# One-hot slot matrix of the expert stages: from GpSimd and VectorE to VectorE alone, with routing and sending two slots closer

## The chip, the cores and the metric

One Trainium2 chip, one of its cores. The metric is the device time of one execution in microseconds (us). The kernel before: median 2519.32 us of 3 executions (2517.7 to 2520.26).

## What is computed

The program is a small transformer on `x` of 32 batches x 256 tokens x 128 features: a binarised feed-forward, a gated attention unit, the same feed-forward again, a mixture of experts, a linear attention, and the mixture of experts again. The change touches the two expert stages only. Cut to what matters, per batch:

```python
logits = layernorm(x) @ router_w + router_b                  # 8 experts
top2, ei = top_k(logits, 2); p = softmax(top2)
pos = running count of tokens per expert, first choices ahead of second ones
inputs[e, pos] += token          # capacity 76 rows per expert; the rest is dropped
h = silu((inputs @ w_fc + b_fc) * (inputs @ w_gate + b_gate))
out = h @ w_proj + b_proj
x = x + 0.5 * sum over the two choices of p * out[ei, pos]
```

## The kernel before, in words

`program` runs six stages one behind the other: ffn, gau, ffn, moe, lin, moe. Within a stage five engines run instruction lists written out by hand and meet at semaphores; each engine takes its list strictly in order. VectorE, ScalarE, GpSimd and SyncE work on what TensorE makes, and a wait at the head of an engine's list holds all that stands behind it.

`moe_stage` (L1286 on) cuts the 32 batches into eight chunks of 2, 3, 5, 5, 5, 5, 5 and 2 batches (`CHUNKS`, here chunk 0 to chunk 7). All batches of a chunk go through the eight experts together, 76 columns each, so five batches make matmuls 380 wide. A chunk is eight units (experts) of four slots, 32 slots in all. In each slot TensorE runs `up` (L1531 on): four matmul instructions of the first weight (L1538) and of the gate weight (L1542), two each; ScalarE adds the first bias (`bias_fc`, L1611), VectorE adds the gate bias and multiplies (`multiply`, L1715), ScalarE takes Silu over two slots' worth (L1618). Behind the fourth slot of a unit TensorE runs `down` for the unit before it (L1552, 24 matmuls for five batches, 16 for two or three) and VectorE adds the output bias (`bias_out`, L1724). The banks for the gate result are two, so the gate matmul of a slot waits for the `multiply` of the slot two before it.

While a chunk is computed, the batches of the next one are routed, and those of the chunk before are gathered and combined. `slots_of` (L1369 on) lays this side work into the slots: batch i of the next chunk starts at slot i times 5 (9 in chunks 0 and 6), and its steps come so many slots later as `ROUTE_LAGS` says:

- norm 0: VectorE normalises (L261), and GpSimd's `split` makes three bf16 parts (L1436 to L1439);
- transpose 1 (L1493, ScalarE's copy L1588), router 2 (matmul L1500; VectorE's `choose` L1662 to L1668), mask 3 (`choose_masks`, L1678 to L1684), count 4 (matmuls L1510 to L1514);
- assign 5: VectorE's `assign` (L1691 to L1700) works out the slot number of both choices of each token (L1697 signals `routed`);
- with assign, GpSimd's `first_choice` (L1442 on, instruction L1447): for each of the two 128-token tiles a `tensor_scalar` over 608 slot numbers, 1 where the number is that of the first choice;
- hot0 at 8 and hot1 at 9: VectorE's `second_choice` (L1702 on, instruction L1705), one tile each: a `scalar_tensor_tensor` that adds the second choice to what GpSimd wrote;
- send0 at 10 and send1 at 11: TensorE's `send` (L1517 on, matmuls L1526, six for each half) moves the tokens into their slots. send0 waits for both tiles of the batch (`hot_sb`); ScalarE's `land` (L1602) copies each half out of the one bank.

In a slot VectorE's order is: multiply, norm, router, mask, assign, hot0 or hot1, combine, and bias_out at the end of a unit. TensorE's order is: up, router, transpose, count, send, down. GpSimd's order is: split, first_choice, gather. `combine` (L1733, then statistics L273) of a batch of the chunk before comes at slots 11, 17, 23 in chunk 2 and 11, 16, 21, 26, 31 in chunks 3 to 6 (14 and 20 in chunk 1), with the four indirect DMAs of its gather (L1456) five slots earlier. In chunk 7 nothing is routed. At the head of a stage chunk 0's two batches are routed with no expert work beside them.

In what follows, the slot of a batch's assign is called A, and the three slots behind it B, C and D. For batch i of chunks 1 to 5 that is A = 5 + 5i.

```python
ROUTE_LAGS = {"norm": 0, "transpose": 1, "router": 2, "mask": 3, "count": 4, "assign": 5, "hot0": 8, "hot1": 9,
              "send0": 10, "send1": 11}
...
if h == 0:
    pe.wait_ge(split_done, b + 1)
    pe.wait_ge(hot_sb, TILES * (b + 1))
```

## Time and profile before

| | us |
|---|---|
| median of 3 executions | 2519.32 |
| the profiled execution, its own time | 2514.78 |
| span of the profile | 2512.8 |
| first expert stage, from its first instruction to the statistics of its last batch | about 514 to 1080 |
| second expert stage | about 1917 to the end |

The profile lists busy time by engine, the span in slices, the chain that ended last, and groups of instructions with the idle time before them and its releaser; the trace gives the instructions in order of time. PE is TensorE, DVE VectorE, ACT ScalarE, POOL GpSimd. A number in square brackets behind an instruction is the idle time of its engine just before it, with what ended it.

### The profile page before, as it was taken

The page shows a single profiled execution, that of the slowest core. Times are in us where ns is not written, and L with a number is a line of the kernel's source. Part 1 is how long each engine was busy: PE and PEld are TensorE (multiplying, and loading weights), DVE is VectorE, ACT ScalarE, POOL GpSimd, SP SyncE. Part 2 cuts the span into 40 slices and gives each one's busy share as a digit, 9 for nine tenths or more (in the row PEclk, how much of TensorE's full clock was granted, in tenths as well). Part 3 has the DMA queues.
Part 4 walks back from the last instruction along what each step waited for, and adds up shares of the span by engine and source line. Part 5 has one row for each costly group of instructions (what it writes and reads, how often), then busy time and mean ns, then how long its engine had stood idle before and what let it go on. Part 6 is the DMA issues. An engine that isn't in the chain of part 4 may idle for free.

```text
span 2512.8 us, 47937 instructions
## 1 busy us (share of the span) xinstructions
PE 2272.8 (90%) x14854; PEld 1816.3 (72%) x14854; DVE 1588.7 (63%) x4974; ACT 1312.6 (52%) x2713; POOL 733.7 (29%) x818
## 2 busy tenths in 40 slices
PE   3979998968999999849999999999996889999994
PEld 3979997957767676637777777777775776776773
DVE  5867776766667775435655656565655666767653
ACT  3755556744444444326666666666662544444441
POOL 2202220045546765320000000000002455766543
PEclk9989999989999999879999999999998999999997
DMA  7040000000111111100000000000000001111122
GB/s 242 0 159 0 0 0 0 0 5 23 26 28 40 41 36 41 46 18 1 0 0 0 0 0 0 0 0 0 0 0 0 15 25 35 43 50 45 49 56 50
DMA packets 70867, 67.45 MB, mean 27 GB/s; under 512 B 9696, under 2 KB 58336, under 8 KB 70368
## 3 DMA queue, kind: packets, MB, share of 16 engines
q1 hardware_dynamic: 61504, 47.16, 5.9%
q0 software_dynamic: 8192, 16.79, 2.9%
q10 hardware_dynamic: 1056, 2.10, 0.3%
q8 instruction: 56, 0.92, 0.2%
q14 instruction: 59, 0.48, 0.1%
HBM read 31.94 MB, written 34.08 MB: 26 GB/s over the span
## 4 chain that ended last, share of the span: by engine, by line
PE 48%; issue 4%; DVE 2%; POOL 1%; ACT 1%; DMA 0%; another core or an unknown queue 0%; ACTq 0%; POOLq 0%; DVEq 0%
PE moe_bank L1552 5%; PE lin_bank L983 5%; PE moe_bank L1538 5%; PE lin_bank L903 5%; PE moe_bank L1542 5%; PE lin_bank L911 4%; PE lin_bank L930 4%; PE lin_bank L922 4%; PE lin_bank L959 3%; PE lin_bank L975 2%; PE moe_bank L1526 2%; PE lin_bank L946 1%; POOL moe_landed L1456 1%; ACT lin_xT L1049 0%; PE moe_bank L1493 0%
## 5 line engine op out<-in xcount | busy, mean ns | idle before, releaser
L1611 ACT ACTIVATE moe_fc<-moe_bank,all_b_fc 128x380 f32<-128x380 f32 (+2 forms) x512 | 262.3, 513 | 341.7 <-PE moe_bank L1538 286.8
L1715 DVE SCALAR_TENSOR_TENSOR moe_act<-moe_bank,all_b_moe_gate,moe_fc 128x380 f32<-128x380 f32 (+2 forms) x512 | 271.0, 531 | 221.4 <-PE moe_bank L1542 106.9
L1538 PE MATMUL moe_bank<-moe_rowsT,all_w_fc 128*128 128x380 f32 (+2 forms) x1024 | 357.3, 431 | 15.6 <-ACT moe_fc L1611 12.8
L1542 PE MATMUL moe_bank<-moe_rowsT,all_w_gate 128*128 128x380 f32 (+2 forms) x1024 | 351.7, 425 | 12.9 <-DVE moe_act L1715 7.7
L1552 PEld LDWEIGHTS moe_bank<-all_w_proj,moe_act 128*128 128x128 f32 x2688 | 321.6, 195 | 12.4 <-ACT moe_act L1618 1.8
L1552 PE MATMUL moe_bank<-all_w_proj,moe_act 128*128 128x128 f32 x2688 | 329.2, 279 | 1.4 <-ACT moe_act L1618 1.4
L1456 POOL DMA_INDIRECT moe_landed<-rows_out,moe_take_at x256 | 266.0, 1039 | 176.2 <-issue 174.6
L1542 PEld LDWEIGHTS moe_bank<-moe_rowsT,all_w_gate 128*128 128x128 f32 x1024 | 188.3, 193 | 101.6 <-DVE moe_act L1715 8.9
L1447 POOL TENSOR_SCALAR moe_hot<-all_slot_ids,moe_slot 128x608 bf16<-128x608 f32 x128 | 233.3, 1830 | 91.7 <-issue 54.9
L1618 ACT ACTIVATE moe_act<-moe_act 128x760 f32<-128x760 f32 (+2 forms) x256 | 181.5, 709 | 96.0 <-DVE moe_act L1715 88.8
L1148 POOL COPY lin_xn_ones<-lin_xn 128x254 f32<-128x254 f32 x32 | 12.7, 398 | 748.0 <-PE lin_bank L911 743.3
L1053 ACT ACTIVATE lin_neg<-lin_bank 128x512 f32<-128x512 f32 x256 | 151.7, 592 | 95.3 <-PE lin_bank L903 50.7
L1538 PEld LDWEIGHTS moe_bank<-moe_rowsT,all_w_fc 128*128 128x128 f32 x1024 | 167.9, 193 | 43.6 <-ACT moe_fc L1611 13.5
L959 PEld LDWEIGHTS lin_bank<-lin_kv,lin_qT 128*128 128x128 f32 x1024 | 144.4, 191 | 63.4 <-issue 54.1
L1057 ACT ACTIVATE lin_neg<-lin_neg 128x512 f32<-128x512 f32 x256 | 161.1, 630 | 7.9
L1526 PE MATMUL moe_bank<-moe_hot,moe_parts 128*128 128x304 bf16 x768 | 125.5, 301 | 40.4 <-issue 24.7
L1081 ACT ACTIVATE lin_gate_tanh<-lin_bank,all_bg_half 128x256 f32<-128x256 f32 x256 | 103.5, 468 | 108.3 <-PE lin_bank L930 108.2
L1724 DVE TENSOR_TENSOR moe_expert_out<-moe_bank,all_b_proj 128x384 f32<-128x384 f32 (+1 forms) x128 | 64.8, 506 | 142.9 <-PE moe_bank L1552 108.4
L959 PE MATMUL lin_bank<-lin_kv,lin_qT 128*128 128x130 f32 x1024 | 151.9, 275 | 1.1 <-DVE lin_heads L1196 0.8
L1526 PEld LDWEIGHTS moe_bank<-moe_hot,moe_parts 128*128 128x128 bf16 x768 | 72.5, 100 | 96.3 <-issue 69.1
L903 PE MATMUL lin_bank<-all_wk,lin_xT 128*128 128x512 f32 x256 | 128.9, 607 | 4.5 <-ACT lin_xT L1049 2.7
L451 ACT ACTIVATE ffn_hT<-ffn_bank,all_b,all_alpha 128x256 f32<-128x256 f32 x256 | 123.6, 564 | 17.2 <-PE ffn_bank L407 17.2
(222 smaller groups left out, 4309.2 us busy)
## 6 DMA issues: line engine op xcount, KB each, us to landing
rows_out<-moe_expert_out SPq DMA_DIRECT2D x80, 128.0 KB
rows_out<-all_zeros SPq DMA_DIRECT2D x1, 9728.0 KB, 28.0
rows_out<-moe_expert_out SPq DMA_DIRECT2D x80, 62.0 KB
moe_landed<-rows_out,moe_take_at POOLq DMA_INDIRECT x256
out<-all_x SPq DMA_DIRECT2D x5, 640.0 KB
rows_out<-moe_expert_out SPq DMA_DIRECT2D x48, 64.0 KB
all_w_fc<-in_w_fc SPq DMA_DIRECT2D x1, 2048.0 KB, 9.8
all_w_gate<-in_w_gate SPq DMA_DIRECT2D x1, 2048.0 KB, 13.7
```

The costliest lines, as they stand in the source:

```text
L903: nc.tensor.matmul(bank[j][:, :], xT[:, j // 2 * P:(j // 2 + 1) * P], k.wk[:, j % 2 * HU:(j % 2 + 1) * HU], start=True, stop=True).then_in ...
L959: last = nc.tensor.matmul(bank[4 + n % 2][:, i * 2 * DH1:(i + 1) * 2 * DH1], qT[:, p, t * P:(t + 1) * P], kv[:, p, :], start=True, stop=True)
L1057: nc.scalar.activation(neg[:, j, :], neg[:, j, :], ACT.Exp, scale=-1.0).then_inc(exps.sem, 1)
L1447: nc.gpsimd.tensor_scalar(hot[:, b % 2, t, :], k.slot_ids[:, :], slot[:, b % 2, t, 0:1], None, ALU.is_equal).then_inc(hot_first, 1)
L1456: nc.gpsimd.indirect_dma_start(landed[:, b % LANDED, t, h, :], None, k.rows_out, bass.IndirectOffsetOnAxis(take_at[:, i, h:h + 1], 0), bou ...
L1526: last = nc.tensor.matmul(bank[SENT][:, 0:HALF], parts[:, b % PARTS, q, t, :], hot[:, b % 2, t, h * HALF:(h + 1) * HALF], start=(t == 0 an ...
L1538: nc.tensor.matmul(bank[FC + j % 2][:, 0:c.width], k.w_fc[:, e, j * P:(j + 1) * P], rowsT[:, c.n % 2, e, 0:c.width], start=True, stop=True ...
L1542: nc.tensor.matmul(bank[GATE + j % 2][:, 0:c.width], k.w_gate[:, e, j * P:(j + 1) * P], rowsT[:, c.n % 2, e, 0:c.width], start=True, stop= ...
L1552: last = nc.tensor.matmul(bank[OUT][:, j * DIM:(j + 1) * DIM], act_in[:, i % 2, h, j * P:(j + 1) * P], k.w_proj[:, e * MC + h, :], start=( ...
L1611: nc.scalar.activation(fc[:, j, 0:c.width], bank[FC + j % 2][:, 0:c.width], ACT.Identity, bias=k.b_fc[:, e * MC + j:e * MC + j + 1]).then_ ...
L1618: nc.scalar.activation(a, a, ACT.Silu).then_inc(act_sb, 1)
L1715: nc.vector.scalar_tensor_tensor(act_in[:, i % 2, j, 0:c.width], bank[GATE + j % 2][:, 0:c.width], k.b_moe_gate[:, e * MC + j:e * MC + j + ...
```

## The change

`first_choice` leaves GpSimd, with its semaphore. VectorE makes each tile whole: a `tensor_scalar` for the first choice, a wait for its own result, and the `scalar_tensor_tensor` as before. The lags of hot0, hot1, send0 and send1 fall from 8, 9, 10, 11 to 6, 7, 8, 9.

```diff
-ROUTE_LAGS = {... "assign": 5, "hot0": 8, "hot1": 9,
-              "send0": 10, "send1": 11}
+ROUTE_LAGS = {... "assign": 5, "hot0": 6, "hot1": 7,
+              "send0": 8, "send1": 9}
...
-                def first_choice(b):
-                    pool.wait_ge(routed, b + 1)
-                    if b >= 2:
-                        pool.wait_ge(sent_ps, 2 * (b - 2) + 2)
-                    for t in range(TILES):
-                        nc.gpsimd.tensor_scalar(hot[:, b % 2, t, :], k.slot_ids[:, :], slot[:, b % 2, t, 0:1], None,
-                                                ALU.is_equal).then_inc(hot_first, 1)
...
                     dve.wait_ge(chosen, b + 1)
                     if b >= 2:
-                        dve.wait_ge(hot_first, TILES * (b - 1))
...
-                def second_choice(b, t):
-                    dve.wait_ge(hot_first, TILES * b + t + 1)
+                def choices(b, t):
                     dve.wait_ge(routed, b + 1)
+                    if b >= 2:
+                        dve.wait_ge(sent_ps, 2 * (b - 2) + 2)
+                    link(nc.vector.tensor_scalar(hot[:, b % 2, t, :], k.slot_ids[:, :], slot[:, b % 2, t, 0:1], None, ALU.is_equal))
                     nc.vector.scalar_tensor_tensor(hot[:, b % 2, t, :], k.slot_ids[:, :], slot[:, b % 2, t, 1:2], hot[:, b % 2, t, :],
                                                    ALU.is_equal, ALU.add).then_inc(hot_sb, 1)
```

The calls of `first_choice` at the head of the stage and with every assign go too, and those of `second_choice` become `choices`. `link` makes VectorE wait for the instruction just issued.

## Rows read from the trace of the kernel before

**Rows 1.** The page, busy time of three engines (share of the span) and instructions.

```profile
PE 2272.8 (90%) x14854; PEld 1816.3 (72%) x14854; DVE 1588.7 (63%) x4974; ACT 1312.6 (52%) x2713; POOL 733.7 (29%) x818
```

**Rows 2.** Busy time in windows, chunk 3, from multiply of A to multiply of D.

```profile
core 0: us, PE busy (x) PEld busy (x) DVE busy (x) ACT busy (x) POOL busy (x), PEclk, DMA share, GB/s
739.25:746.68 7.43, 7.42 (x43) 5.50 (x42) 4.95 (x21) 3.57 (x6) 5.77 (x6) 1.00 0.01 3
749.71:758.88 9.17, 8.99 (x55) 7.01 (x56) 7.20 (x28) 4.18 (x8) 8.37 (x9) 1.00 0.18 42
...
776.66:783.38 6.72, 6.72 (x38) 4.86 (x37) 6.41 (x27) 3.65 (x7) 5.20 (x6) 1.00 0.10 29
788.17:796.49 8.32, 8.32 (x49) 6.25 (x50) 5.54 (x19) 4.02 (x7) 6.84 (x6) 1.00 0.13 28
```

**Rows 3.** Timeline of DVE, slots A to D of batch i = 3.

```profile
776.66 0.61 DVE L1715 SCALAR_TENSOR_TENSOR moe_act<-moe_bank,all_b_moe_gate,moe_fc 128x380 f32<-128x380 f32 x1 [0.82 <-PE moe_bank L1542]
777.19 0.60 DVE L261 TENSOR_SCALAR moe_xn<-all_x,moe_mean,moe_rstd 128x128 f32<-128x128 f32 x2
...
779.32 0.61 DVE L1715 SCALAR_TENSOR_TENSOR moe_act<-moe_bank,all_b_moe_gate,moe_fc 128x380 f32<-128x380 f32 x1
779.85 1.82 DVE L1733 SCALAR_TENSOR_TENSOR all_x<-moe_landed,moe_prob,all_x 128x128 f32<-128x128 f32 x4
...
782.10 0.60 DVE L1715 SCALAR_TENSOR_TENSOR moe_act<-moe_bank,all_b_moe_gate,moe_fc 128x380 f32<-128x380 f32 x1
...
783.38 0.59 DVE L1715 SCALAR_TENSOR_TENSOR moe_act<-moe_bank,all_b_moe_gate,moe_fc 128x380 f32<-128x380 f32 x1
```

**Rows 4.** Timeline of PE beside it: gates of A and D, one send.

```profile
775.72 0.80 PE L1542 MATMUL moe_bank<-moe_rowsT,all_w_gate 128*128 128x380 f32 x2
...
778.63 0.94 PE L1526 MATMUL moe_bank<-moe_hot,moe_parts 128*128 128x304 bf16 x6
...
781.76 0.80 PE L1542 MATMUL moe_bank<-moe_rowsT,all_w_gate 128*128 128x380 f32 x2
```

**Rows 5.** Instructions by tile (ns min/median/max), and the page's group of bias_out.

```profile
L1447 POOL TENSOR_SCALAR moe_hot<-all_slot_ids,moe_slot x128: 1790/1812/2090, 527.9 to 2401.1; 128x608 bf16<-128x608 f32 x128
L1705 DVE SCALAR_TENSOR_TENSOR moe_hot<-all_slot_ids,moe_slot,moe_hot x128: 836/844/1355, 529.8 to 2406.9; 128x608 bf16<-128x608 f32 x128
...
L773 DVE TENSOR_SCALAR gau_lin_qT<-gau_qkT,all_os_gamma,all_os_beta x33: 408/412/414, 169.4 to 386.0; 128x256 f32<-128x256 f32 x33
...
L261 DVE TENSOR_SCALAR moe_xn<-all_x,moe_mean,moe_rstd x128: 331/341/479, 520.6 to 2386.1; 128x128 f32<-128x128 f32 x128
...
L1724 DVE TENSOR_TENSOR moe_expert_out<-moe_bank,all_b_proj 128x384 f32<-128x384 f32 (+1 forms) x128 | 64.8, 506 | 142.9 <-PE moe_bank L1552 108.4
```

**Rows 6.** Timeline of DVE: a combine with no first_choice beside it.

```profile
691.71 1.25 DVE L1733 SCALAR_TENSOR_TENSOR all_x<-moe_landed,moe_prob,all_x 128x128 f32<-128x128 f32 x4
```

**Rows 7.** Busy time in windows: batch i = 3 of chunk 1, batch 0 of chunk 0.

```profile
626.32:633.12 6.80, 4.67 (x30) 3.77 (x29) 6.26 (x27) 2.99 (x7) 6.38 (x7) 1.00 0.15 38
...
547.48:550.99 3.51, 3.51 (x31) 3.43 (x30) 2.46 (x12) 1.89 (x5) 1.98 (x2) 1.00 0.01 2
```

**Rows 8.** Timeline of PE: three waits in chunk 1, with what followed the first.

```profile
613.51 1.31 PE L1526 MATMUL moe_bank<-moe_hot,moe_parts 128*128 128x304 bf16 x6 [2.24 <-issue]
614.61 3.26 PE L1552 MATMUL moe_bank<-all_w_proj,moe_act 128*128 128x128 f32 x16
...
622.84 2.03 PE L1552 MATMUL moe_bank<-all_w_proj,moe_act 128*128 128x128 f32 x16
...
2017.90 0.94 PE L1526 MATMUL moe_bank<-moe_hot,moe_parts 128*128 128x304 bf16 x6 [2.18 <-issue]
...
2036.39 0.65 PE L1542 MATMUL moe_bank<-moe_rowsT,all_w_gate 128*128 128x228 f32 x2 [3.39 <-DVE moe_act L1715]
```

**Rows 9.** Busy time in a window behind the first of these waits.

```profile
614.00:616.00 2.00, 2.00 (x11) 1.80 (x10) 1.97 (x8) 0.92 (x2) 0.00 (x0) 0.50 0.03 8
```

**Rows 10.** Timeline of PE: the first send of the stage.

```profile
533.04 1.68 PE L1526 MATMUL moe_bank<-moe_hot,moe_parts 128*128 128x304 bf16 x6 [6.01 <-DVE moe_hot L1705]
```

More of the change, by code:

```diff
@@ L1262 @@
 COMBINE_IN = {1: (14, 6), 2: (11, 6), 3: (11, 5), 4: (11, 5), 5: (11, 5), 6: (11, 5), 7: (12, 6)}
-ROUTE_LAGS = {"norm": 0, "transpose": 1, "router": 2, "mask": 3, "count": 4, "assign": 5, "hot0": 8, "hot1": 9,
-              "send0": 10, "send1": 11}
+ROUTE_LAGS = {"norm": 0, "transpose": 1, "router": 2, "mask": 3, "count": 4, "assign": 5, "hot0": 6, "hot1": 7,
+              "send0": 8, "send1": 9}
 GATHER_LEAD = 5
@@ L1341, in moe_stage @@
         routed = k.sem("routed")
-        hot_first = k.sem("first_choice_hot")
         hot_sb = k.sem("hot_ready")
@@ L1467, in _ @@
                     split(b)
-                for b in plan[0].batches:
-                    first_choice(b)
                 for c, slots in order:
@@ L1473, in _ @@
                             split(work["norm"])
-                        if "assign" in work:
-                            first_choice(work["assign"])
                         if "gather" in work:
@@ L1746, in _ @@
                     for t in range(TILES):
-                        second_choice(b, t)
+                        choices(b, t)
                 dve.wait_ge(cleared, 1)
@@ L1762, in _ @@
                             if f"hot{t}" in work:
-                                second_choice(work[f"hot{t}"], t)
+                                choices(work[f"hot{t}"], t)
                         if "combine" in work:
```

## The prediction

> **What bounds the kernel now.** I read the page first: TensorE is busy 90% of the span, VectorE 63%, GpSimd 29% [rows 1]. So a whole-span view says that VectorE has room and GpSimd more. But the change puts work into particular slots, so what counts is which engine is behind in those. I took windows of chunk 3 that run from the multiply of slot A to that of slot D, four of its five routed batches [rows 2] (the fifth, i = 2, is like i = 1). TensorE is busy in all of them nearly without a gap (8.99 of 9.17 us, 6.72 of 6.72): any wait that it gets there is added to the time one for one. The granted clock is 1.00, that is 2.4 GHz. VectorE is busy 4.95, 7.20, 6.41 and 5.54 us in the same windows, on the bare busy count.
>
> Then the timeline of batch 3 [rows 3, 4]. VectorE's multiply of A starts at 776.66, 0.14 us after the gate matmul of A ends (775.72 + 0.80). It works from there to 783.38 with no idle time, and at D it is already behind: TensorE's gate of D ended at 782.56. Today that costs nothing, since nothing at D needs VectorE at once; its two hots come in D and E and the send in the next A.
>
> **What the change moves.** send0 moves from the next A to D, and it needs both tiles of the batch, which VectorE now makes in B and C, at the full price of two instructions. All that VectorE has in A, B and C stands ahead: multiply, norm, assign; multiply, first tile, combine with statistics; multiply, router, second tile. TensorE goes from the gate of A to send0 with two sends fewer, as those moved on to D and E. So per batch two sums are compared, and where VectorE's is the longer TensorE waits.
>
> VectorE's additions, per tile. The `scalar_tensor_tensor` takes 0.84 us [rows 5], of which the next instruction overlaps some 0.08 (multiply at 776.66 lasts 0.61, the next starts at 777.19) [rows 3]: 0.76. The `tensor_scalar` of 608 elements on VectorE is not in the trace. Nearest rows: `tensor_scalar` of 128 elements takes 0.341 us and of 256 elements 0.412 [rows 5], so 0.55 ns an element and 0.61 us for 608. Those have two per-partition operands and this one has one, so I take 0.58, and 0.04 for the wait on its own result. The other end is 0.84, the `scalar_tensor_tensor` over the same 608. Together 1.38 us a tile, 2.76 a batch, the new one 1.24 of it.
>
> The slope of 0.55 ns is half the cycle-per-element cost that separates the two instruction kinds here. The Trainium skill (VectorE: DVE Perf Modes, section "The perf-mode tier table") has fp32 `tensor_scalar` from SBUF to SBUF at 2 elements a cycle and two-tensor operations at 1. By that page's overhead figure of about 150 cycles the tile's `tensor_scalar` would be an estimated 0.47 us, and the sum below some 12 us smaller; the rows have no instruction that short at this size.
>
> What VectorE gets back: GpSimd's two instructions of 1.81 us a batch [rows 5] run beside the combine today. The combine of batch 3 takes 1.82 us [rows 3], one with none beside it 1.25 [rows 6]: 0.5 us back in B. Against it, GpSimd's split (norm's consumer) is still running when B begins, and the first `tensor_scalar` can be held by it; bounds 0 and the 0.6 us by which the combine was held, I take 0.4 (0.25 for i = 2, where the addition of the output bias comes between).
>
> Now the sums for chunks 2 to 5, in us. VectorE before is the busy time plus 0.3 for the short gaps between linked instructions (6.72 less 6.41). Added are 2.76, 0.14 for the start, the 0.4, less the 0.5; in i = 0 and i = 4 the addition of the output bias, 0.5 [rows 5], falls behind the second tile and is taken off; i = 0 has no combine, and i = 4 no norm and so no split. TensorE is the window less 1.88 for two sends of 0.94 [rows 4] (i = 0 has none of them).
> - i = 0: 5.2 - 0.5 + 3.3 = 8.0 against 7.4: wait 0.6.
> - i = 1: 7.5 + 2.8 = 10.3 against 7.3: 3.0.
> - i = 2: as i = 1, with 0.25 for the 0.4: 2.8.
> - i = 3: 6.7 + 2.8 = 9.5. TensorE from 776.52 to 782.56 is 6.04, less 1.88 is 4.2: wait 5.3. No `down` lies between A and D here; in the other four one of 2.8 us does, which is the difference.
> - i = 4: 5.8 - 0.5 + 2.9 - 0.5 = 7.7 against 6.4: 1.3.
>
> Sum 13.0, less some 0.3 for short waits that stand at sends today: 12.7 us a chunk, 4 chunks, 2 stages: **102 us**. After each send0 VectorE has only mask and multiplies until the next A, so it catches up, and the wait comes anew with each batch.
>
> Chunk 1, with 228 columns: same steps; the largest is again i = 3, whose A also has a combine: VectorE 6.26 + 2.9 = 9.2, TensorE 4.67 - 1.88 = 2.8 [rows 7], wait 6.4. The five together make 13. Today's waits there (2.24 and its clock loss, about 2 at i = 3, smaller ones; 2.18 and 3.39 in the second stage) [rows 8] are taken in by the new order, about 7: net 6 a stage, **12 us**. These rows also show the mechanism at work before the change: a combine in the slot of hot1 (14) or of assign (20) stops TensorE. Chunk 0: VectorE 2.5 + 0.3 + 2.9 = 5.7, at 0.3 less for the others, TensorE 3.5 [rows 7]: 2.0 for three batches, less 0.7 that I estimate for today's short waits there: 5.3 a stage, **11 us**. Chunk 6 has nine slots a batch and no combine ahead of the tiles: 0, at best 1 us back.
>
> Head of a stage: the first send waits 6.01 us for the matrix [rows 10], behind two tiles at GpSimd's 1.81 and one 0.84 addition, 4.5 us; now 2 x 1.4 behind both assigns: 0.9 earlier, **-2 us** in all.
>
> **Clock.** After the 2.24 us wait the granted clock was 0.50 (1.2 GHz) for some 3 us [rows 9]; the send took 1.31 us in place of 0.94 and the `down` 3.26 in place of 2.03 [rows 8]: 1.6 to 1.7 us lost. After waits of 2.18 and 3.39 us it was not: that send took its 0.94. So I charge 1.7 for each wait over 5 us, ten of them (i = 3 in chunks 1 to 5, twice): **17 us**. Bounds: nothing, and all 26 waits over 2.5 us, 44.
>
> The moved sends cost the same matmuls; GpSimd's list only gets shorter; SyncE's is untouched; ScalarE's `land` waits behind send0 and is released in time, 0.41 us before the next half needs the bank against TensorE's four `up` matmuls of 1.3. Landing two slots earlier gains nothing: no row has TensorE wait for the rows of a chunk. The dropped wait for `hot_first` was for work long done.
>
> Sum: 102 + 12 + 11 - 2 + 17 = **140 us** on the profiled execution's 2514.8, thus 2655. The median of the runs is 4.5 us above that execution, so 2659.
>
> **Rivals.**
> 1. Faster: VectorE takes the additions in its idle time (37% of the span) and what shows is GpSimd's release. It decides where VectorE's sum from A to the second tile stays under TensorE's. Then 0.5 us back in each combine is off the path, and 2 us at the heads, today's waits in chunk 1 (about 7 a stage, 14) remain: 2519 - 16 = 2503. For it: the page's shares. Against: in i = 3 VectorE is behind at D even before. The same rule of ports stands in the Trainium skill (SBUF — State Buffer, "SBUF: two separate sides"): the port pair shared by VectorE and GpSimd is held exclusively for a whole instruction; by that rule, the 1.82 against 1.25 agrees. Chance 0.04; another 0.02 that it comes out level.
> 2. The waits come, but the clock stays: 2659 - 17 = 2642. Chance 0.25.
> 3. The waits come only where no `down` lies between (i = 3), as VectorE's chain is shorter than summed by 1.5 us or more: 8 x 3.8, 2 x 5 in chunk 1, 10 for the clock: +50, 2569. Chance 0.09.
> 4. The `tensor_scalar` runs at one element a cycle, 0.84, or is held by GpSimd's gathers as long: 0.26 to 0.3 more a tile, 0.55 a batch, in 28 batches a stage: +31, 2690; with the clock's upper bound 2715. For it: two-operand instructions of this size do, and no row has a compare that writes bf16. Chance 0.18.
>
> The forecast itself has 0.42. The matrix made by VectorE is plainly in the diff, so "does nothing" is no rival.
>
> **How the numbers follow.** 2659 is the forecast's own sum. The range leaves out rival 1, the level case and most of rival 3, and runs to the upper bound of rival 4: 2595 to 2715. A measurement can tell 0.2% (5 us) from no change: faster 0.04, same 0.02, slower 0.94.
>
> **What would show it.** In the new profile TensorE's L1526 should have some 60 long waits for VectorE's hot, 5 us ones where no `down` precedes; VectorE's idle time in A to C should be gone and the combine near 1.25 us; GpSimd's busy time down by 233 us. Right about the price if the new `tensor_scalar` is 0.5 to 0.65 us. Wrong if TensorE's waits at L1526 sum to under 50 us, or if the time comes back from another place, as matmuls at the lower clock.

## The result and the profile after

| | before | after |
|---|---|---|
| median (4 executions each), us | 2519.24 (2517.7 to 2520.26) | 2672.9 (2670.31 to 2675.66) |
| profiled execution, us | 2514.78 | 2674.94 |
| its span, us | 2512.8 | 2672.8 |
| granted TensorE clock, mean | 0.967 | 0.944 |

The ratio is 1.0619, with a 95% interval of 1.0605 to 1.0633. Slower by 154 us by the medians; the two spans differ by 160.0. Forecast was 2659 in a range of 2595 to 2715: the sign, the size and the mechanism came out, with one term missing (chunk 6) and three that were off (the clock too small, chunk 2 and the waits of chunks 3 to 5 too large). That the total lies so close is in part luck.

The lines of code moved up by 9 to 14: fc L1525, gate L1529, down L1539, send L1513, multiply L1703, bias_out L1712, combine L1721, gather L1447, the counting matmul L1497. The new `tensor_scalar` on VectorE is L1692, the `scalar_tensor_tensor` behind it L1693.

The page of after, busy time by engine, and its group for the sends:

```profile
PE 2324.1 (87%) x14854; PEld 1849.5 (69%) x14854; DVE 1642.5 (61%) x5102; ACT 1312.1 (49%) x2713; POOL 506.2 (19%) x690
...
L1513 PE MATMUL moe_bank<-moe_hot,moe_parts 128*128 128x304 bf16 x768 | 143.9, 332 | 159.3 <-issue 146.0
```

Against [rows 1]: GpSimd lost 227.5 us, VectorE gained 54 (its 128 new instructions, less what the combines got back), and TensorE, with exactly the same 14854 matmuls, is busy 51 us longer. The matmuls are the same, so what grew is the time of each, and the granted clock fell from 0.967 to 0.944 on the mean. VectorE's share of the span fell, to 61%, in a kernel that it holds up: the share says nothing here.

The waits of TensorE in after (engine, line, releaser: us in total, times, longest):

```profile
PE moe_bank L1513 <- issue: 146.0, 56, 12.5
...
PE moe_bank L1513 <- DVE moe_hot L1693: 10.0, 2, 5.0
PE moe_bank L1497 <- DVE moe_mask L1666: 9.5, 10, 1.9
PE moe_bank L1529 <- DVE moe_act L1703: 9.3, 6, 2.3
```

There are the "some 60 long waits" at the send: 56 of them, which the profile books under "issue" (it names no releaser), 48 of 0.9 us or more and 8 of 0.3. That they are waits for VectorE's second tile has to be read from the timelines. The timeline of VectorE in after, slots A to D of batch i = 3 of chunk 3, which answers to [rows 3]:

```profile
807.98 0.61 DVE L1703 SCALAR_TENSOR_TENSOR moe_act<-moe_bank,all_b_moe_gate,moe_fc 128x380 f32<-128x380 f32 x1 [0.82 <-PE moe_bank L1529]
...
809.66 0.67 DVE L1681 SCALAR_TENSOR_TENSOR moe_over<-moe_top_atf,moe_over 128x4 f32<-128x4 f32 x1
...
811.00 0.61 DVE L1703 SCALAR_TENSOR_TENSOR moe_act<-moe_bank,all_b_moe_gate,moe_fc 128x380 f32<-128x380 f32 x1
811.53 0.53 DVE L1692 TENSOR_SCALAR moe_hot<-all_slot_ids,moe_slot 128x608 bf16<-128x608 f32 x1
812.09 0.85 DVE L1693 SCALAR_TENSOR_TENSOR moe_hot<-all_slot_ids,moe_slot,moe_hot 128x608 bf16<-128x608 f32 x1
812.86 1.25 DVE L1721 SCALAR_TENSOR_TENSOR all_x<-moe_landed,moe_prob,all_x 128x128 f32<-128x128 f32 x4
...
815.82 0.52 DVE L1692 TENSOR_SCALAR moe_hot<-all_slot_ids,moe_slot 128x608 bf16<-128x608 f32 x1
816.37 0.85 DVE L1693 SCALAR_TENSOR_TENSOR moe_hot<-all_slot_ids,moe_slot,moe_hot 128x608 bf16<-128x608 f32 x1
817.14 0.61 DVE L1703 SCALAR_TENSOR_TENSOR moe_act<-moe_bank,all_b_moe_gate,moe_fc 128x380 f32<-128x380 f32 x1
```

Nine microseconds with no idle time: from 807.98 to 817.22, 9.2 us, or 9.4 with the 0.14 of start that the forecast's 9.5 includes. The timeline of TensorE beside it, the gates of slots A and D and every send0 of that chunk that waited over 0.9 us, with what followed:

```profile
784.14 0.94 PE L1513 MATMUL moe_bank<-moe_hot,moe_parts 128*128 128x304 bf16 x6 [2.52 <-issue]
...
800.72 0.94 PE L1513 MATMUL moe_bank<-moe_hot,moe_parts 128*128 128x304 bf16 x6 [3.37 <-issue]
...
807.04 0.80 PE L1529 MATMUL moe_bank<-moe_rowsT,all_w_gate 128*128 128x380 f32 x2
...
811.80 0.80 PE L1529 MATMUL moe_bank<-moe_rowsT,all_w_gate 128*128 128x380 f32 x2
...
817.33 1.68 PE L1513 MATMUL moe_bank<-moe_hot,moe_parts 128*128 128x304 bf16 x6 [4.72 <-issue]
...
818.80 4.81 PE L1539 MATMUL moe_bank<-all_w_proj,moe_act 128*128 128x128 f32 x24
...
829.51 2.84 PE L1539 MATMUL moe_bank<-all_w_proj,moe_act 128*128 128x128 f32 x24
...
834.60 0.94 PE L1513 MATMUL moe_bank<-moe_hot,moe_parts 128*128 128x304 bf16 x6 [0.97 <-issue]
```

TensorE had its gates of A to D done at 812.60 and stood until 817.33, 0.11 us behind VectorE's second tile. What follows runs slow: the send 1.68 in place of 0.94, the `down` 4.81 in place of 2.84. The windows of after show why (columns as in [rows 2]; the last but two is the granted clock):

```profile
818.00:820.00 2.00, 2.00 (x10) 1.74 (x9) 0.33 (x3) 0.96 (x2) 1.39 (x3) 0.50 0.15 33
...
784.00:790.00 6.00, 5.86 (x27) 3.52 (x28) 1.58 (x7) 2.17 (x6) 0.09 (x1) 0.72 0.06 12
```

Half clock, 1.2 GHz, behind the wait of 4.72; and 0.72 on the mean over the six microseconds behind the wait of only 2.52.

**Where the time went.** A chunk with five batches behind it and five ahead, from its first multiply to that of the next, is the cleanest unit of the stage. Windows of that length, chunk 4 of the first stage, before:

```profile
806.30:883.60 77.30, 75.89 (x446) 54.52 (x445) 55.84 (x185) 36.60 (x68) 50.46 (x50) 1.00 0.14 38
```

and after:

```profile
844.20:936.40 92.20, 80.34 (x446) 57.22 (x445) 59.99 (x196) 36.71 (x68) 33.10 (x40) 0.94 0.13 32
```

The chunk grew by 14.9 us: 10.4 of it TensorE standing (11.86 against 1.41), and 4.5 the same 446 matmuls taking longer (80.34 against 75.89). By chunk, first stage, in us, from the first multiplies in the timelines:

| chunk | 0 | 1 | 2 | 3, 4, 5 | 6 |
|---|---|---|---|---|---|
| before | 45.4 | 64.2 | 78.1 | 77.3 each | 69.1 |
| after | 50.3 | 73.5 | 84.7 | 92.2 each | 82.3 |
| grown by | 4.9 | 9.3 | 6.6 | 14.9 each | 13.2 |

That is 78.7 of the 79.3 by which the first stage grew. The second grew by 78.5 in nearly the same pattern (6.4, 8.0 and 6.5 in chunks 0 to 2, 14.5 to 15.1 in chunks 3 to 5, 13.2 in chunk 6), and the first stage began 2.0 us later than in the trace of before, which the change has no part in: 79.3 + 78.5 + 2.0 is the 160 of the spans.

Chunk 6 was forecast at nothing. Its growth is for the most part one stop. Timeline of TensorE in after:

```profile
1059.19 2.84 PE L1539 MATMUL moe_bank<-all_w_proj,moe_act 128*128 128x128 f32 x24
1061.87 0.81 PE L1525 MATMUL moe_bank<-moe_rowsT,all_w_fc 128*128 128x380 f32 x2
...
1077.26 1.68 PE L1513 MATMUL moe_bank<-moe_hot,moe_parts 128*128 128x304 bf16 x6 [12.47 <-issue]
```

of VectorE:

```profile
1074.51 0.56 DVE L1712 TENSOR_TENSOR moe_expert_out<-moe_bank,all_b_proj 128x384 f32<-128x384 f32 x1 [9.34 <-remote]
```

and of ScalarE:

```profile
1074.55 1.04 ACT L1598 ACTIVATE moe_fc<-moe_bank,all_b_fc 128x380 f32<-128x380 f32 x2 [9.84 <-remote]
```

VectorE and ScalarE both stood still for more than nine microseconds, up to the same moment, and the views name no engine for it ("remote"). The semaphore events of the trace, which no view prints, do: ScalarE waited for the signal of an `up` matmul and VectorE for that of the `down`, both TensorE's. The `down` ends at 1062.03 by its record and its signal came at 1074.48, 12.45 us later; the `up` of 1061.87 ends at 1062.67 and its signal came at 1074.53. In the expert stages such a signal comes 0.014 us behind the recorded end in the median, and at most 0.015 in nine of ten. So the stop is TensorE's: its work or its signals came late, and which of the two can't be told, as the profile only models where a matmul ends. It turned into a wait of 12.47 us because VectorE's list is in order: the second tile stands behind `bias_out`, and `bias_out` waits for the `down`. The clock followed, and the send took 1.68.

On GpSimd at that time a train of sixteen indirect DMAs was going out, 1.3 us apart, from 1051.66 to 1072.55. Rows from its start and its end:

```profile
1051.66 1.03 POOL L1447 DMA_INDIRECT moe_landed<-rows_out,moe_take_at  x1 [0.77 <-POOL moe_parts L1438]
1053.00 1.00 POOL L1447 DMA_INDIRECT moe_landed<-rows_out,moe_take_at  x1 [0.30 <-issue]
...
1071.55 1.00 POOL L1447 DMA_INDIRECT moe_landed<-rows_out,moe_take_at  x1 [0.30 <-issue]
```

In the kernel before, GpSimd makes its tiles between two gathers, and for that it must first wait for VectorE's assign. Timeline of GpSimd before, chunk 6 and then chunk 7:

```profile
988.88 1.01 POOL L1456 DMA_INDIRECT moe_landed<-rows_out,moe_take_at  x1 [0.30 <-issue]
993.02 3.61 POOL L1447 TENSOR_SCALAR moe_hot<-all_slot_ids,moe_slot 128x608 bf16<-128x608 f32 x2 [3.13 <-DVE moe_slot L1697]
996.80 1.10 POOL L1456 DMA_INDIRECT moe_landed<-rows_out,moe_take_at  x1 [0.17 <-issue]
...
1011.75 1.00 POOL L1456 DMA_INDIRECT moe_landed<-rows_out,moe_take_at  x1 [0.30 <-issue]
...
1038.23 0.99 POOL L1456 DMA_INDIRECT moe_landed<-rows_out,moe_take_at  x1 [25.49 <-issue]
...
1057.76 1.00 POOL L1456 DMA_INDIRECT moe_landed<-rows_out,moe_take_at  x1 [0.30 <-issue]
```

There the longest train of chunk 6 is one of twelve (996.80 to 1012.75), and no stop comes with it (the second stage has one of 2.2 us there). But chunk 7, where nothing is routed and GpSimd has nothing to wait for, has a train of sixteen in the kernel before too, and there VectorE stops the same way:

```profile
1061.10 0.42 DVE L1724 TENSOR_TENSOR moe_expert_out<-moe_bank,all_b_proj 128x256 f32<-128x256 f32 x1 [4.58 <-remote]
```

The change took GpSimd's wait out with the work, and chunk 6 has a train of sixteen as well. Whether that is the cause, runs had to say.

### The profile page after: what moved, and what is told of

It is laid out like the page before. It is cut to its first block, busy times and chain, and to the rows that moved or that the text cites. A ratio compares the mean times of both kernels' runs of the same rounds, so it can differ in the third digit from the quotient of the medians.

```text
span 2672.8 us, 47839 instructions
## 1 busy us (share of the span) xinstructions
PE 2324.1 (87%) x14854; PEld 1849.5 (69%) x14854; DVE 1642.5 (61%) x5102; ACT 1312.1 (49%) x2713; POOL 506.2 (19%) x690
## 4 chain that ended last, share of the span: by engine, by line
PE 47%; issue 5%; DVE 2%; ACT 1%; POOL 1%; another core or an unknown queue 0%; ACTq 0%; DMA 0%; POOLq 0%; DVEq 0%
PE moe_bank L1539 6%; PE moe_bank L1525 5%; PE moe_bank L1529 5%; PE lin_bank L983 5%; PE lin_bank L903 4%; PE lin_bank L911 4%; PE lin_bank L930 4%; PE lin_bank L922 4%; PE lin_bank L959 3%; PE moe_bank L1513 3%; PE lin_bank L975 2%; PE lin_bank L946 1%; POOL moe_landed L1447 1%; PE moe_bank L1480 0%; ACT lin_xT L1049 0%
## 5 line engine op out<-in xcount | busy, mean ns | idle before, releaser
L1703 DVE SCALAR_TENSOR_TENSOR moe_act<-moe_bank,all_b_moe_gate,moe_fc 128x380 f32<-128x380 f32 (+2 forms) x512 | 271.4, 531 | 300.7 <-PE moe_bank L1529 172.3
L1525 PE MATMUL moe_bank<-moe_rowsT,all_w_fc 128*128 128x380 f32 (+2 forms) x1024 | 360.7, 435 | 16.7 <-ACT moe_fc L1598 10.9
L1529 PE MATMUL moe_bank<-moe_rowsT,all_w_gate 128*128 128x380 f32 (+2 forms) x1024 | 358.6, 433 | 11.0 <-DVE moe_act L1703 9.3
L1539 PEld LDWEIGHTS moe_bank<-all_w_proj,moe_act 128*128 128x128 f32 x2688 | 342.6, 206 | 15.3 <-ACT moe_act L1605 1.6
L1539 PE MATMUL moe_bank<-all_w_proj,moe_act 128*128 128x128 f32 x2688 | 347.6, 289 | 1.3 <-ACT moe_act L1605 0.7
L1447 POOL DMA_INDIRECT moe_landed<-rows_out,moe_take_at x256 | 275.5, 1076 | 257.3 <-issue 118.4
L1513 PE MATMUL moe_bank<-moe_hot,moe_parts 128*128 128x304 bf16 x768 | 143.9, 332 | 159.3 <-issue 146.0
L1529 PEld LDWEIGHTS moe_bank<-moe_rowsT,all_w_gate 128*128 128x128 f32 x1024 | 191.2, 196 | 101.9 <-DVE moe_act L1703 15.1
L1513 PEld LDWEIGHTS moe_bank<-moe_hot,moe_parts 128*128 128x128 bf16 x768 | 74.7, 107 | 223.6 <-issue 190.7
L1525 PEld LDWEIGHTS moe_bank<-moe_rowsT,all_w_fc 128*128 128x128 f32 x1024 | 170.7, 196 | 45.2 <-ACT moe_fc L1598 11.6
L1589 ACT COPY moe_rowsT<-moe_bank 128x304 f32<-128x304 f32 x128 | 52.8, 412 | 266.8 <-PE moe_bank L1513 256.7
L1712 DVE TENSOR_TENSOR moe_expert_out<-moe_bank,all_b_proj 128x384 f32<-128x384 f32 (+1 forms) x128 | 64.6, 504 | 175.8 <-PE moe_bank L1539 108.6
L1148 POOL COPY lin_xn_ones<-lin_xn 128x254 f32<-128x254 f32 x32 | 12.7, 398 | 748.2 <-PE lin_bank L911 743.5
L1435 POOL CAST moe_parts<-moe_xn 128x256 bf16<-128x256 f32 x64 | 25.5, 398 | 643.8 <-DVE moe_xn L261 351.4
## 6 DMA issues: line engine op xcount, KB each, us to landing
all_w_gate<-in_w_gate SPq DMA_DIRECT2D x1, 2048.0 KB, 13.2
```

Of the source, the lines that this page charges most:

```text
L1447: nc.gpsimd.indirect_dma_start(landed[:, b % LANDED, t, h, :], None, k.rows_out, bass.IndirectOffsetOnAxis(take_at[:, i, h:h + 1], 0), bou ...
L1513: last = nc.tensor.matmul(bank[SENT][:, 0:HALF], parts[:, b % PARTS, q, t, :], hot[:, b % 2, t, h * HALF:(h + 1) * HALF], start=(t == 0 an ...
L1525: nc.tensor.matmul(bank[FC + j % 2][:, 0:c.width], k.w_fc[:, e, j * P:(j + 1) * P], rowsT[:, c.n % 2, e, 0:c.width], start=True, stop=True ...
L1529: nc.tensor.matmul(bank[GATE + j % 2][:, 0:c.width], k.w_gate[:, e, j * P:(j + 1) * P], rowsT[:, c.n % 2, e, 0:c.width], start=True, stop= ...
L1539: last = nc.tensor.matmul(bank[OUT][:, j * DIM:(j + 1) * DIM], act_in[:, i % 2, h, j * P:(j + 1) * P], k.w_proj[:, e * MC + h, :], start=( ...
L1703: nc.vector.scalar_tensor_tensor(act_in[:, i % 2, j, 0:c.width], bank[GATE + j % 2][:, 0:c.width], k.b_moe_gate[:, e * MC + j:e * MC + j + ...
```

## The experiments

Two theories went in. **Mine**: VectorE's chain from A to the second tile is longer than TensorE's work up to D, so the short lags cost most, and the extra VectorE work little by itself. **The rival**: the extra VectorE work costs wherever the send stands. Beside them two smaller questions: the stop in chunk 6, and the clock. Ratios are to the kernel before on the same chip; single executions where no interval is given. "Chunk" is the length of one of chunks 3 to 5 of the first stage as above. The experiments ran on three chips: e1, e2, e3 and e5 on one, e4, e6, e7 and e8 on a second, e9 to e12 on a third. The expected times in us of the first eight were written with the 2519 us of the first table in mind; the ratios show better whether they came true.

**e1_old_lags.** The matrix by VectorE, the places of before.

```diff
-"assign": 5, "hot0": 6, "hot1": 7, "send0": 8, "send1": 9}
+"assign": 5, "hot0": 8, "hot1": 9, "send0": 10, "send1": 11}
```

> The changed kernel with the four lags put back to 8, 9, 10, 11; VectorE still makes the whole matrix, GpSimd none. Theory (the chain of VectorE work between slot A and send0 is what TensorE waits for, and the short lags made it so): the two tiles fall into D and E, TensorE has one more slot and two sends between A and send0 (about 11.9 us against 11.7 of VectorE work), so the waits of 2.5, 3.3, 4.7 us at L1526's counterpart are gone and nearly all of the +160 us with them; 2515 to 2545 us, the upper part if the two stops of some 9.8 us of ScalarE and VectorE at a train of gathers in chunk 6 stay. Rival (the added VectorE work as such costs the time, wherever it stands): above 2600 us.

2597.74 against 2522.64, 1.0298: between the two. A chunk took 83.8, and send0 waited 1.64, 1.59, 0.95 and 1.48 us in it where before had 0.45, 0.49 and 0.34. So I had left out a cost of the work itself. Another 1.92 us is a wait of one send1, right behind a "remote" stop of ScalarE of 3.7 us at a train of eight gathers. ScalarE's stops of this kind at `bias_fc` sum to 53.2 us here, before 26.2. e7 has the same places on a chip without such stops.

**e2_short_lags_gpsimd.** The other half alone: the kernel before, with the places of after.

```diff
-"assign": 5, "hot0": 8, "hot1": 9, "send0": 10, "send1": 11}
+"assign": 5, "hot0": 6, "hot1": 7, "send0": 8, "send1": 9}
```

> The kernel before with only the lags cut to 6, 7, 8, 9; GpSimd still makes the first choice. Theory (lags alone): GpSimd's split and two first choices end some 6.7 us after the gate of A, VectorE stands waiting for the first of them in B with combine and multiply queued behind it, and the second tile is ready no earlier than in the changed kernel (9.5 us after A): waits at send0 as long or longer, 2640 to 2700 us; chunk 6 has no stop of ScalarE and VectorE, as GpSimd still waits for each assign. Rival (VectorE's new instruction is the cost): VectorE does 1.1 us a batch less, so under 2600 us.

2741.9, 1.0869, a chunk of 99 to 100; 56 waits at the send, 179.9 us. That is above the range of 2640 to 2700, and the stops in chunk 6 were not gone (4.9 us at most): a train of twelve goes with them here. The short lags alone cost more than the whole change: GpSimd's two tiles, 3.6 us behind assign, are then in the chain too. Given the short lags, making the matrix on VectorE is the better of the two.

**e3_paced_gathers.** After, with the wait for assign put back on GpSimd where `first_choice` stood.

```diff
+if "assign" in work:
+    pool.wait_ge(routed, work["assign"] + 1)
```

> The changed kernel, with GpSimd waiting for the batch's assign where it used to make the first choice, and doing nothing then. Theory (the 12.5 and 11.8 us waits of TensorE in chunk 6 come from gathers that run ahead in one train since GpSimd no longer waits there): they go, together with their stretch at the lower clock: 2640 to 2652 us. Rival (these stops have nothing to do with GpSimd's pacing): 2673 us within 4.

2656.41, 1.0530 where after has 1.0619; the expected range ended at 2652. The 12.5 us wait is gone, the longest at the send is 4.7, and chunk 6 of the first stage took 73.6 in place of 82.3; chunks 3 to 5 stayed (92.8). The waits of ScalarE in after:

```profile
ACT moe_fc L1598 <- remote: 48.5, 10, 9.8
```

and in this run:

```profile
ACT moe_fc L1600 <- remote: 31.7, 8, 5.6
```

The longest train in chunk 6 is one of twelve again. So what the missing wait let loose costs 8.7 of chunk 6's 13.2 us. After itself was not profiled on this chip, but e5, with the gathers let loose, took 83.5 there, so the chip doesn't make the 8.7. The other 4.5 is not explained by the wait: stops of up to 5.0 us remain, at the train of twelve.

**e5_double_first.** The suspected price twice: the `tensor_scalar` of each tile is issued two times.

```diff
+link(nc.vector.tensor_scalar(hot[:, b % 2, t, :], k.slot_ids[:, :], slot[:, b % 2, t, 0:1], None, ALU.is_equal))
```

> The changed kernel with the new tensor_scalar on VectorE issued twice for each tile, 128 more instructions of 0.53 us and a wait each. Theory (VectorE's chain to send0 is the bound in some 26 of 30 batches a stage): 1.1 us more in each of those waits, 55 to 65 us, and more waits long enough to lower the clock, up to 40 us more: 2728 to 2775 us. Rival (the send is bound by something else, and VectorE has slack): under 2690 us.

2779.18, 1.1017, just above the expected 2775. A chunk went from 92.2 to 102.4, 10.2 for ten more instructions of 0.56 us from start to start: more than the 5.6 of their own time. Each of the five waits grew by 1.15 us (0.28, 2.52, 3.26, 4.73 and 0.97 to 1.43, 3.67, 4.41, 5.88 and 2.12), which makes 5.7: the chain is the bound one for one in the waits. The other 4.5 are matmuls that take longer, with more time at the lower clock (mean 0.931 where after had 0.944).

**e4_filled_waits** (16 calls of a 128-column matmul with no use, ahead of the wait of i = 3 alone) and **e12_all_waits_filled** (8, 11 and 16 calls ahead of those of i = 1, 2 and 3). They add TensorE work and take none away; if the time falls, it is the clock. The edit of e12:

```diff
+FILL = (0, 8, 11, 16, 0)
...
+c = chunk_of(b)
+if 2 <= c.n <= 6:
+    for _ in range(FILL[b - c.batches[0]]):
+        nc.tensor.matmul(bank[ROUTE + b % 2][:, 384:512], k.ident[:, :], k.ident[:, :], start=True, stop=True)
```

> The changed kernel, with 16 fp32 matmuls of 128 columns (32 instructions, 3.8 us) on the identity into unused columns of a bank, put ahead of the wait of send0 for the batch i = 3 of chunks 1 to 5 alone, where TensorE waits 4.7 us. They add work and no one reads them. Theory (part of the loss is TensorE's clock, which falls to 0.50 behind these waits): the clock stays at 1.00 there, the send takes 0.94 in place of 1.68 and the down 2.84 in place of 4.81, 2.7 us less in each of 8 to 10 places: 2643 to 2655 us. Rival (the clock costs nothing by itself): 2673 within 4, or more if the added work gets in the way.

> The changed kernel with matmuls nobody reads ahead of send0 in i = 1, 2 and 3 of chunks 1 to 5 (16, 22 and 32 instructions: 1.9, 2.6 and 3.8 us against waits of 2.5, 3.3 and 4.7). With i = 3 alone filled, a chunk fell only from 92.2 to 91.1 us, as the clock then fell behind the wait of i = 1 instead. Theory (the lower clock costs some 3 us a chunk in all): the clock stays at 1.00 through chunks 3 to 5 and a chunk lasts 88.5 to 90 us. Rival (the filling costs what the clock gives): 91 to 93 us.

e4: 2608.73 against 2492.45, 1.0467, but on a chip where the expert stages show no stop by "remote" (chunk 6: 68.0 with GpSimd's list as in after), so its ratio isn't to be set beside 1.0619. Its chunk is 91.1, only 1.1 less. The clock stayed up behind i = 3, fell behind i = 1 as it does in after, and fell behind i = 2 as well, where after has 1.00 (chunk 3, first row i = 1, then i = 2):

```profile
778.00:782.00 4.00, 3.60 (x14) 2.15 (x15) 1.23 (x6) 1.04 (x3) 0.35 (x1) 0.57 0.21 33
...
795.00:799.00 4.00, 4.00 (x19) 2.31 (x18) 0.83 (x6) 1.81 (x4) 0.00 (x0) 0.57 0.07 16
```

With all three filled, e12, it is 88.6, and 1.0506. Its chunk 4:

```profile
834.00:923.00 89.00, 84.24 (x517) 62.72 (x517) 59.96 (x195) 36.84 (x69) 33.21 (x40) 1.00 0.13 33
```

Seventy more matmul instructions, a granted clock of 1.00 over the chunk, and the chunk 3.6 us shorter. The lower clock thus costs 3.6 us a chunk by this run, which pays a little for the filling, and 4.5 by the busy time above.

**e8_combine_moved.** After, with the combines of chunks 3 to 6 at slots 13, 18, 23, 28 and 31, out of the slot of the first tile.

```diff
+at = (13, 18, 23, 28, 31)[i] if 3 <= c.n <= 6 else first + i * gap_of
```

> The changed kernel, with the combines of chunks 3 to 6 moved from slots 11, 16, 21, 26, 31 to 13, 18, 23, 28, 31, that is from B to D, and their gathers with them. Theory: 1.9 to 2.1 us of VectorE work leave the chain ahead of send0 in four batches a chunk (to 0.4, 1.2, 2.6, 0 us of wait), and the clock no longer falls: 7 to 10 us a chunk for chunks 3 to 5 in two stages, 45 to 60 us: 2610 to 2630 us. Rival (combine is not in that chain): 2673 within 5.

2564.33, 1.0288, a chunk of 82.1: 10.1 us back, for four combines with statistics of 1.7 us that leave the chain, and the clock with them (1.00 over chunk 4, in which the longest wait is 3.05). The waits are 0.3, 1.2, 1.6, 3.1 and 0: TensorE stands 5.7 us less, and its matmuls take 4.4 less. Where the same wait of 3.05 lowered the clock, as in chunk 5, the chunk is 83.7, and those of the second stage are 83.4 to 83.7.

**e6_lags_7_to_10.** One slot later each.

```diff
+"assign": 5, "hot0": 7, "hot1": 8, "send0": 9, "send1": 10}
```

> The changed kernel with lags 7, 8, 9, 10: the tiles in C and D, send0 in E. Theory: one down of 2.84 us now lies between A and send0 in every batch, VectorE's chain grows by a multiply, the mask and the output bias to 11.1 us against TensorE's 9.2 with one send: about 1.5 to 2 us of wait for the batches with a combine and no fall of the clock there: 2570 to 2605 us. Rival (a threshold: any lag below the old one costs the same): 2650 or more.

2579.26, 1.0348, a chunk of 85.4 (up to 87.2 in the second stage). The sends wait about 1.1 each; a new wait stands at the counting matmul for the mask, 37.9 us in 30 times, where after has 9.5: VectorE's tiles now fall right ahead of the next batch's masks.

**e7_old_lags_paced.** e1 and e3 together: the old places, VectorE's matrix, the gathers held back. Five executions.

> Old lags 8 to 11, the matrix by VectorE alone, GpSimd waiting for each assign without work. Theory: VectorE has 0.8 us of slack left at send0, the combines are shorter by 0.5 us since no first choice holds them, the head of each stage is 1 us earlier and the gathers are paced: as the kernel before or better by a few us, 2505 to 2522 us. Rival (GpSimd's first choice was worth having, as VectorE's extra 1.1 us a batch shows up in the narrow chunks): 2525 to 2545 us.

2544.13 against 2492.45, 1.0202 (1.0188 to 1.0216): more than the theory and the rival had, who gave at most 1.010. Its chunk is 81.3, and the sends wait:

```profile
844.50 0.93 PE L1515 MATMUL moe_bank<-moe_hot,moe_parts 128*128 128x304 bf16 x6 [1.65 <-issue]
...
857.85 0.94 PE L1515 MATMUL moe_bank<-moe_hot,moe_parts 128*128 128x304 bf16 x6 [1.59 <-issue]
...
884.46 0.94 PE L1515 MATMUL moe_bank<-moe_hot,moe_parts 128*128 128x304 bf16 x6 [0.64 <-issue]
...
896.72 0.93 PE L1515 MATMUL moe_bank<-moe_hot,moe_parts 128*128 128x304 bf16 x6 [1.49 <-issue]
```

The second tile stands in the slot right ahead of send0, and in the kernel before there is no room left between them: its sends wait 0.3 to 0.5 us already. The 1.1 us that VectorE's work grew by in that batch goes on the path at once, with the old places too. I had thought of 0.8 us of room there. The four waits make the whole difference between 81.3 and the 77.3 of before; the chip has no part in it, as the waits of e4, e8 and after agree from chip to chip to some 0.1 us. Chunk 6 took 73.0, though this chip has no stops and e4, with nothing held back, took 68.0 there; so that holding the gathers back has a price of its own is not ruled out.

**e10_tiles_early_send_late.** If the place decides and not the engine, VectorE's matrix must be almost free with the tiles early (lags 6, 7), the sends late (10, 11), the combines one slot before the next A, and the gathers held back. Five executions.

```diff
+"assign": 5, "hot0": 6, "hot1": 7, "send0": 10, "send1": 11}
+at = (14, 19, 24, 29, 31)[i] if c.n < 7 else first + i * gap_of
```

> VectorE makes the whole matrix, tiles in B and C as in the change (lags 6, 7), but send0 and send1 stay at 10 and 11, the combines of chunks 1 to 6 stand in E (14, 19, 24, 29, the fifth at 31), and GpSimd waits for each assign. Theory (it is the place of the work against the send, not the engine): no wait of over 1 us at send0 in chunks 2 to 5, a chunk of five batches lasts 77 to 78.5 us as in the kernel before; ratio 0.993 to 1.006. Rival (VectorE's added 1.1 us a batch costs wherever it stands, as with the old lags): 1.015 to 1.022.

2529.4 against 2516.93, 1.0040 (1.0025 to 1.0055). A chunk of 77.6, before 77.3, with all of VectorE's new work in it:

```profile
804.00:882.00 78.00, 76.03 (x448) 55.05 (x447) 60.41 (x196) 37.10 (x69) 32.28 (x40) 1.00 0.15 38
```

VectorE is busy 60.41 us there and TensorE is idle for 2.0. Chunks 1 and 2 of the first stage (62.1 and 76.7) are shorter than before; what is left is chunk 6, 78.1 where before took 69.1, with its stops: with the gathers moved, its train is of sixteen again in spite of the wait (991.5 to 1012.5).

**e11_after_again.** After once more, unchanged, on the chip of e9, e10 and e12. Four executions.

> The changed kernel as it is, on the chip of these runs. On the chip of e4 to e8 the kernel before takes 2492 us in place of 2519 and shows none of the stops of ScalarE and VectorE that the profile puts down to no engine. Theory (those stops belong to a chip, and the wait at send0 to the kernel): if this chip is of that sort, chunks 3 to 5 last 92.2 us each as before, the 12.5 us wait in chunk 6 is gone, and the ratio falls to 1.045 to 1.056. Rival (the ratio is the same on any chip): 1.060 to 1.064.

2671.59 against 2516.93, 1.0612 (1.0595 to 1.0629); chunk 92.1, the longest wait 11.8, ScalarE's "remote" 48.7. All of it repeats on another chip.

**e9_before_combine_spread.** The kernel before, with the combines of chunks 1 and 2 out of the slots that stop TensorE [rows 7, 8]. Eleven executions.

```diff
-COMBINE_IN = {1: (14, 6), 2: (11, 6), ...
+COMBINE_IN = {1: (16, 5), 2: (11, 5), ...
```

> The kernel before with one line changed: the combines of chunk 1 at 16 and 21 in place of 14 and 20, those of chunk 2 at 11, 16, 21 in place of 11, 17, 23, so that none stands in the slot of hot1, assign or mask. Theory: TensorE's waits of 2.2 and 2.0 to 3.4 us in chunk 1 and of 1.1 in chunk 2 go, with one stretch at the lower clock: 5 to 7 us a stage, 0.995 to 0.997 of the kernel before. Rival (the waits move to the next send): 0.999 to 1.001.

2512.57 against 2516.93, 0.9981 (0.9972 to 0.9990): 0.2% faster than the kernel before, between the theory (0.995 to 0.997) and the rival (0.999 to 1.001). The waits of 2 and 3 us in chunk 1 are gone (longest at the send 1.2), but chunk 1 of the first stage took 66.0 against 64.2 and chunk 2 76.4 against 78.1, so this profile doesn't show where the gain lies; it is of the slowest of the eleven, 2517.23. It stays open.

Chunks 3 to 5 of the first stage in all of these, in us, side by side: before 77.3; tiles early and sends late 77.6; old places 81.3 (83.8 with the stops of e1); combine moved 82.1; one slot later 85.4; three waits filled 88.6; one wait filled 91.1; after 92.2; gathers paced 92.8; short lags with GpSimd 99.4; `tensor_scalar` twice 102.4.

## Why the forecast was right, and where not

- **VectorE's chain against TensorE's work in A to D**: right. Waits forecast for i = 0 to 4: 0.6, 3.0, 2.8, 5.3, 1.3; found 0.3, 2.5, 3.3, 4.7, 1.0. Net of what stood there before, 12.7 a chunk was forecast and 10.4 found. e5 (longer chain, longer chunk) and e8 (shorter chain, 10 us back) show that it is this chain. For i = 3 the 0.6 us too much lie in TensorE's sum, not in VectorE's: from the end of A's gate to that of D's it took 4.76 us (807.84 to 812.60), where the forecast had 6.04 less two sends of 0.94, 4.2. A send lasts 0.94, but the next matmul starts 0.77 behind its start (778.63 and 779.40 in the trace of before), so two sends that move away give back 1.5 at most, and 1.3 was found.
- **The price of the new instruction**: the tile view of after has

```profile
L1692 DVE TENSOR_SCALAR moe_hot<-all_slot_ids,moe_slot x128: 514/527/939, 531.2 to 2560.4; 128x608 bf16<-128x608 f32 x128
L1693 DVE SCALAR_TENSOR_TENSOR moe_hot<-all_slot_ids,moe_slot,moe_hot x128: 850/851/854, 531.7 to 2561.0; 128x608 bf16<-128x608 f32 x128
```

  0.53 us, forecast 0.58; a tile takes 1.33 from start to start of what follows (811.53 to 812.86), forecast 1.38. Rival 4 is out. (Its upper end, by the forecast's own terms, is 2690 + 44 - 17 = 2717 and not 2715.) The Trainium skill (VectorE: DVE Perf Modes, section "The perf-mode tier table") has fp32 `tensor_scalar` at twice the rate of two-tensor operations; 0.53 against 0.85 over the same 608 elements agrees, and so with a bf16 result. The estimate of 0.47 us from its overhead figure is 0.05 too short.
- **0.4 us for being held by GpSimd's split**: here it was `assign` that took longer beside the split (0.67 us at 809.66, for 128x4 elements, where the one behind it takes 0.17), not the first tile. A long hold of the `tensor_scalar` is rare (939 ns at most, 527 in the median). The combine did come back from 1.82 to 1.25.
- **The clock, 17 us**: right that a wait costs clock, too low in size. "I charge 1.7 for each wait over 5 us" failed as a rule: no wait of these chunks reaches 5 us, and behind 4.72 and behind 2.52 us it fell. Forecast 1.7 us a chunk, found 3.6 (e12) to 4.5 (busy time): in the six chunks of this kind, three in each stage, 11 to 17 us more. Rival 2, no loss at all, is out.
- **Chunk 2 counted like chunks 3 to 5**: wrong. Its combines come at 11, 17 and 23, of which only the first stands between an assign and the second tile (in a slot VectorE makes the tile ahead of the combine). Its waits are 0.3, 2.5, 1.6, 3.0 and 0, from i = 2 on those of e8, which has no combine in these slots; it grew by 6.6, where 14.4 (12.7 and 1.7) was forecast. In two stages some 16 us too much.
- **Chunks 0 and 1, heads**: 4.9 and 9.3 in the first stage, 6.4 and 8.0 in the second, forecast 5.3 and 7.7 (6 and the clock's 1.7); the first wait of a stage fell from 6.01 to 5.02 as forecast. The 6.4 us of i = 3 in chunk 1 came as two waits, 2.33 at the gate, which with two banks waits for the multiply of two slots before, and 3.17 at the send.
- **Chunk 6, "0, at best 1 us back"**: wrong by 13.2 us in each stage. The step that failed is "GpSimd's list only gets shorter": the removed work carried a wait, and without it the longest train of indirect DMAs in chunk 6 grew from twelve to sixteen. e3 shows that 8.7 us hang on it. On the chip of e4 and e8 that step held: chunk 6 took 68.0 and 68.1 us with the same train, 1 us less than the 69.1 of before. The forecast's own test, GpSimd's busy time down by 233, found 227.5, and could not show this.
- **What the work costs where it stood**: the forecast didn't need it, but I held the old places to be nearly free, and e7 measured 2.0% for them. Taken in that order, a chunk's 14.9 are 4.0 for VectorE's work at the old places and 10.9 for the short lags. The two don't add up: the short lags alone cost 22 (e2), and VectorE's matrix then gives 7 back.

So the forecast came out 14 us below the measured median, with larger errors that partly cancelled: missing were chunk 6 (26) and the size of the clock's loss (up to 17), too much were chunk 2 (16) and the waits in chunks 3 to 5 (2.3 a chunk, 14). The mechanism of the main term was right; that the sum came within 14 us was luck.

## What to carry to other kernels

Before a step is moved closer to its user, add up what each engine has in its list between the two, slot by slot: an engine that is 63% busy over the span can be the one that is late in just these slots, and the engine that waits also loses clock. When work is taken off a queue, look for the waits that go with it and what they were spacing out. And when an engine waits for one that the profile doesn't name, look for the semaphore and for who raises it. The cheap fix for work that lands in a bad slot is another slot: VectorE carried the whole matrix at 0.4% in e10, with tiles made early, sends late and the combines moved out of their way.

## What had not been expected of the hardware

- The granted clock fell to 0.50 behind waits of 2.52 us in a dense stretch (0.72 over 784 to 790), while behind the wait of 3.37 us the window from 800 to 806 has 1.00. In e8 one and the same wait of 3.05 lowered it in chunks 2 and 5 (0.50 over 723.5 to 726 and 972.5 to 975) and not in 3 and 4. So the length of the wait alone doesn't tell. Filling the waits with matmuls of no use kept it at 1.00 and gained 3.6 us in 92.
- ScalarE and VectorE stopped together for 9.8 and 9.3 us during a train of sixteen indirect DMAs 1.3 us apart. Both waited for signals of TensorE that came up to 12.45 us behind the recorded ends of its matmuls. On the chip where e4 ran, the same train left no such stop and no late signal, and chunk 6 took 68.0 us in place of 82.3. The two other chips of the experiments show such stops in every kernel. In all these traces every signal of TensorE in the expert stages that was over 1 us late came during a run of gathers or within 3 us of its last one. What delays TensorE, and why on some chips only, was not settled.
- The chips differ: the same kernel before took 2492.45, 2516.93 and 2522.64 us on three of them. Hence ratios and chunk lengths, and no times, are compared here.
